# Adding each layer's residual during its last scan, strip by strip, in a four-image convolution block on one core

## Time and profile before

| | |
|---|---|
| median of 3 runs | 2475.09 us (2470.94 to 2479.65) |
| profiled execution | 2475.43 us, span in the trace 2473.6 us |
| PE busy | 2191.7 us (89%) |
| DVE busy | 1443.6 us (58%) |
| ACT busy | 739.2 us (30%) |
| POOL busy | 329.3 us (13%) |
| DMA queue of SP (q1) | 112224 packets, 120.06 MB, 21.1% of the 16 DMA engines' time |

### The profile page before, as it was taken

The page is one execution under the profiler, slowest core; times in us unless marked ns, Lnnn a source line. Parts: engine busy times, 40 slices in busy tenths (PEclk is TensorE's granted clock), DMA queues, the critical chain, the costliest instruction groups (busy, mean ns, idle before and its releaser), DMA issues.

```text
span 2473.6 us, 43617 instructions
## 1 busy us (share of the span) xinstructions
PE 2191.7 (89%) x17396; PEld 1975.7 (80%) x17396; DVE 1443.6 (58%) x3275; ACT 739.2 (30%) x1154; POOL 329.3 (13%) x363
## 2 busy tenths in 40 slices
PE   2999999999999999999999915999999999953786
PEld 2889669489329999999999915999999999952454
DVE  5866776766774444445555586444445555577855
ACT  7923342433545004420035415003440000002442
POOL 2233213123008300000000063000000000000300
PEclk9999999999999999999999967999999999976898
DMA  7600111121355000000000076100000000049935
GB/s 129 107 11 13 16 23 14 17 52 37 58 100 94 1 1 1 1 1 1 1 1 1 1 217 158 22 1 1 1 1 1 1 1 1 1 114 280 304 106 153
DMA packets 119956, 126.72 MB, mean 51 GB/s; under 512 B 50528, under 2 KB 99936, under 8 KB 116960
## 3 DMA queue, kind: packets, MB, share of 16 engines
q1 hardware_dynamic: 112224, 120.06, 21.1%
q10 hardware_dynamic: 7424, 4.06, 0.6%
q0 software_dynamic: 128, 0.01, 0.0%
HBM read 64.47 MB, written 50.33 MB: 46 GB/s over the span
## 4 chain that ended last, share of the span: by engine, by line
PE 83%; DVE 12%; issue 1%; ACT 1%; SPq 1%; DMA 1%; POOL 0%; ACTq 0%; DVEq 0%; POOLq 0%
PE bank L1105 20%; PE bank L1106 18%; PE bank L1107 18%; PE bank L995 10%; PE bank L1066 7%; PE bank L998 4%; DVE stats L1244 4%; PE bank L1069 2%; DVE work L1387 2%; PE bank L1219 2%; PE bank L1010 1%; DVE image L1515 1%; PE bank L1191 1%; DMA band<-in_x 1%; DVE image L1478 1%
## 5 line engine op out<-in xcount | busy, mean ns | idle before, releaser
L1464 DVE TENSOR_TENSOR image<-bank,image 112x128 f32<-112x128 f32 x2032 | 660.4, 325 | 711.4 <-PE bank L1107 711.4
L1105 PE MATMUL bank<-image,scan_area 112*112 112x128 f32 x4064 | 809.5, 280 | 10.4 <-ACT image L849 6.7
L1106 PE MATMUL bank<-image,scan_area 112*112 112x126 f32 x4064 | 771.0, 271 | 0.0
L1107 PE MATMUL bank<-image,scan_area 112*112 112x126 f32 x4064 | 769.7, 270 | 0.0
L1106 PEld LDWEIGHTS bank<-image,scan_area 112*112 112x112 f32 x4064 | 581.3, 176 | 0.0
L1105 PEld LDWEIGHTS bank<-image,scan_area 112*112 112x112 f32 x4064 | 566.3, 175 | 16.2 <-ACT image L849 7.1
L1107 PEld LDWEIGHTS bank<-image,scan_area 112*112 112x112 f32 x4064 | 578.5, 176 | 0.0
L995 PE MATMUL bank<-work 128*128 128x192 f32 x1536 | 307.9, 338 | 28.6 <-DVE work L1387 27.2
L845 ACT COPY work<-image 48x256 f32 x192 | 80.2, 418 | 684.6 <-PE bank L1107 684.3
L995 PEld LDWEIGHTS bank<-work 128*128 128x128 f32 x1536 | 249.9, 194 | 34.2 <-issue 33.1
L783 ACT COPY work<-work 32x1008 f32<-32x1008 f32 x128 | 132.0, 1031 | 298.0 <-PE bank L998 195.1
(11 more groups left out here) (161 smaller groups left out, 1476.4 us busy)
## 6 DMA issues: line engine op xcount, KB each, us to landing
work<-saved SPq DMA_DIRECT2D x64, 384.0 KB, 10.1
saved<-image SPq DMA_DIRECT2D x36, 384.0 KB, 6.9
image<-flat_rows SPq DMA_DIRECT2D x4, 3072.0 KB, 15.9
out<-image SPq DMA_DIRECT2D x8, 1536.0 KB, 8.4
work<-work SPq DMA_DIRECT2D x128, 70.9 KB, 2.8
flat_rows<-image SPq DMA_DIRECT2D x46, 192.0 KB, 5.8
band<-in_x SPq DMA_DIRECT2D x16, 384.0 KB, 5.7
scan_area<-in_x SPq DMA_DIRECT2D x16, 384.0 KB, 5.8
```

Source lines behind the costliest of these rows:

```text
L1105: mm(dst, wt[:, 1], src, start=True, stop=False)
L1106: mm(dst[:, 1:J2, :], wt[:, 0], src[:, 0:J2 - 1, :], start=False, stop=False)
L1107: mm(dst[:, 0:J2 - 1, :], wt[:, 2], src[:, 1:J2, :], start=False, stop=True).then_inc(s_prod[g], 1)
L1464: v.tensor_tensor(line(g, along_w, at), prod, line(g, along_w, src), ALU.add).then_inc(s_state[g], 1)
```

## The change

It does four things. The second exchange is gone: the input of the layer is brought from `saved[0]` in the layout that pass 4 has, in 16 tiles, each a strip of 16 columns j (32 image columns) of one pair and one w, and the sum is made in that layout. As soon as PE has read 8 more columns j of a pair (16 steps; a half strip), POOL adds them to the buffer (112 x 1024 values an add, 28 adds a layer); DVE adds the last half strip after the scan. ACT writes the finished half strips home to `image`: in layer 0 with four 48-partition copies that exchange the layout (`swap_home`), in layer 1 with four 112-partition activations that add the bias and write natural rows (`rows_home`). DVE measures six of the eight half strips inside pass 4, one bn_stats of 128 values after its add in 192 of the 254 slots, beginning 14 steps after the half strip was read, and the last two after the scan. SP saves sums and brings tiles inside pass 4, and in layer 1 it writes each strip of each image to `flat_rows`. Both norms are made once for all four images. The diff, cut to its core:

```diff
-HELD = 2 * (K2 // 8) - GAP
+STRIP = 16
+HALF_STRIP = STRIP // 2
+STRIPS = J2 // STRIP
+TILES = 4 * STRIPS
+LAST = 2 * STRIPS - 1
+PIECE_AT = 14
+ENTRIES = 8 * (LAST - 1) + 4
...
+        def in_image(g, s, half, rows):
+            j = J2 - (half + 1) * HALF_STRIP
+            return image_l[rows, g, s, :, j:j + HALF_STRIP, :].rearrange("p k j b -> p k (j b)")
+        def in_buffer(g, w, half, rows):
+            v = back[(half // 2 * 4 + 2 * g + w) % GAP][rows, :].rearrange("p (k n) -> p k n", k=K2)
+            return v[:, :, (1 - half % 2) * STRIP:(2 - half % 2) * STRIP]
+        def add_half(vector, g, w, half):
+            dst = in_buffer(g, w, half, slice(0, P))
+            return vector.tensor_tensor(dst, in_image(g, w, half, slice(0, P)), dst, ALU.add)
...
             def bring(t):
+                strip, g, w = t // 4, t // 2 % 2, t % 2
+                j = J2 - (strip + 1) * STRIP
+                for h, rows in enumerate((LO, HI)):
+                    src = saved[0][w].rearrange("c (g s k j b) -> c g s k j b", g=2, s=2, k=K2, b=2)
+                    sp.dma_start(back[t % GAP][rows, :].rearrange("p (k n) -> p k n", k=K2),
+                                 src[:, g, h, :, j:j + STRIP, :].rearrange("c k j b -> c k (j b)"))\
+                        .then_inc(s_back[t % GAP], 16)
...
+            for t in range(TILES):
+                summed(sp, t)
+                save(t)
+                if 2 <= t < TILES + 2 - GAP:
+                    done = t - 2
+                    sp.wait_ge(s_gone[done % GAP], 32 * (done // GAP + 1))
+                    sp.wait_ge(s_home, 2 * (done // 4 * 2 + 1) + done // 2 % 2 + 1)
+                    bring(done + GAP)
...
+            def send_rows(strip, b):
+                j = J2 - (strip + 1) * STRIP
+                for h, rows in enumerate((LO, HI)):
+                    sp.dma_start(lines[h, b, :, :, 2 * j:2 * (j + STRIP)],
+                                 image_l[rows, b // 2, b % 2, :, j:j + STRIP, :].rearrange("p k j b -> p k (j b)"))\
+                        .then_inc(s_flat[b], 16)
...
+            for strip in range(STRIPS - 1):
+                for g in range(2):
+                    sp.wait_ge(s_home, HOMES + 2 * (2 * strip + 1) + g + 1)
+                    for t in (4 * strip + 2 * g, 4 * strip + 2 * g + 1):
+                        if t + GAP < TILES:
+                            bring_sum(t + GAP)
+                    send_rows(strip, 2 * g)
+                    send_rows(strip, 2 * g + 1)
+            sp.wait_ge(s_home, 2 * HOMES - 1)
+            send_rows(STRIPS - 1, 0)
+            send_rows(STRIPS - 1, 1)
+            bring_tokens(0)
+            sp.wait_ge(s_home, 2 * HOMES)
+            send_rows(STRIPS - 1, 2)
+            bring_tokens(1)
+            send_rows(STRIPS - 1, 3)
...
-            pool.wait_ge(s_swap, 6 * K2 + 1)
-            for t in range(1, 2 * NBLK, 2):
-                pool.wait_ge(s_back[t % GAP], 32 * (t // GAP + 1))
-                nc.gpsimd.tensor_tensor(dst, piece(image, t), piece(back[t % GAP], t), ALU.add).then_inc(s_kept_p, 1)
+            def add_strips(layer):
+                for half in range(LAST):
+                    for g in range(2):
+                        pool.wait_ge(s_prod[g], (layer * PASSES + 3) * STEPS + 2 * HALF_STRIP * (half + 1))
+                        for w in range(2):
+                            brought(pool, layer, half // 2 * 4 + 2 * g + w)
+                            add_half(nc.gpsimd, g, w, half).then_inc(s_kept_p, 1)
...
+            def swap_home(g, half):
+                for w, to in enumerate((LO, HI)):
+                    for h, of in enumerate((LO, HI)):
+                        last = nc.scalar.copy(in_image(g, h, half, to), in_buffer(g, w, half, of))
+                return last
+            def rows_home(g, half):
+                for b in range(2):
+                    for w in range(2):
+                        dst = in_image(g, b, half, slice(0, P)).rearrange("p k (j w) -> p w k j", w=2)
+                        src = in_buffer(g, w, half, slice(0, P)).rearrange("p k (j b) -> p b k j", b=2)
+                        last = nc.scalar.activation(dst[:, w], src[:, b], ACT.Identity, bias=b2_col[0:P, :], scale=1.0)
+                return last
...
-                with act.Fori(0, K2 - 1) as i:
-                    exchange(True, K2 - 1 - i, 3 * i + n0)
-                exchange(True, 0, n0 + 3 * (K2 - 1))
+                for half in range(LAST + 1):
+                    for g in range(2):
+                        if half < LAST:
+                            act.wait_ge(s_kept_p, layer * 4 * LAST + 4 * half + 2 * g + 2)
+                        else:
+                            act.wait_ge(s_kept_v, layer * 4 + 2 * g + 2)
+                        (rows_home if layer else swap_home)(g, half).then_inc(s_home, 1)
...
                     v.tensor_tensor(line(g, along_w, at), prod, line(g, along_w, src), ALU.add).then_inc(s_state[g], 1)
+                    if scan == PASSES - 1:
+                        strip_piece(layer, 2 * n + g)
+            def strip_piece(layer, slot):
+                half, i = divmod(slot - 2 * PIECE_AT, 4 * HALF_STRIP)
+                half -= 1
+                if not 0 <= half < LAST - 1:
+                    return
+                g, n, b = i // 16, i // 2 % 8, i % 2
+                if i % 16 == 0:
+                    dve.wait_ge(s_home, layer * HOMES + 2 * half + g + 1)
+                v.bn_stats(dst, 128 values of in_image(g, ..., half, ...))
...
+                    add_last(0)
+                    for half in (LAST - 1, LAST):
+                        for g in range(2):
+                            for b in range(2):
+                                for n in range(2):
+                                    last = strip_end(0, g, half, b, n)
+                    group_norm(4, P, ENTRIES)
...
+            add_last(1)
-            for t in range(NBLK):
-                relayout(t)
-            group_norm(6, P, NSTAT, 0, 2)
+            for g in range(2):
+                for half in (LAST - 1, LAST):
+                    dve.wait_ge(s_home, HOMES + 2 * half + g + 1)
+                    for b in range(2):
+                        for n in range(2):
+                            last = strip_end(1, g, half, b, n)
+                last.then_inc(s_taken, 1)
+            group_norm(5, P, ENTRIES)
```

More of the change, by code:

```diff
@@ L276, in build @@
         s_raw = [sem(f"s_raw{i}") for i in range(SAVES)]
-        s_keep = [sem(f"s_keep{g}") for g in range(2)]
+        s_gone = [sem(f"s_gone{i}") for i in range(GAP)]
+        s_home = sem("s_home")
         s_scan_w = sem("s_scan_w")
@@ new lines, in brought, with summed, all_gone @@
+        def brought(eng, layer, t):
+            eng.wait_ge(s_back[t % GAP], 32 * (layer * len(range(t % GAP, TILES, GAP)) + t // GAP + 1))
+        def summed(eng, t):
+            g, w, last = t // 2 % 2, t % 2, t // 4 * 2 + 1
+            eng.wait_ge(s_kept_p, 4 * min(last, LAST - 1) + 2 * g + w + 1)
+            if last == LAST:
+                eng.wait_ge(s_kept_v, 2 * g + w + 1)
+        def all_gone(eng):
+            for i in range(GAP):
+                eng.wait_ge(s_gone[i], 32 * len(range(i, TILES, GAP)))
@@ L1466, in _, with add_last @@
+            def add_last(layer):
+                for g in range(2):
+                    dve.wait_ge(s_state[g], (layer + 1) * PASSES * STEPS + layer + 1)
+                    for w in range(2):
+                        brought(dve, layer, 2 * LAST - 2 + 2 * g + w)
+                        add_half(v, g, w, LAST).then_inc(s_kept_v, 1)
             for layer in range(2):
                 if layer:
-                    def sums(t):
-                        dve.wait_ge((s_kept_v, s_kept_p)[t % 2], t // 2 + 1)
-                        for i in range(2):
-                            for q in range(2):
-                                last = take_stats(P, t // NBLK * 2 + i, t % NBLK * 2 + q, summed(t)[:, i, q])
-                        return last
@@ L1475, in _ @@
-                    for t in range(0, 2 * NBLK, 2):
-                        dve.wait_ge(s_back[t % GAP], 32 * (t // GAP + 1))
-                        dst = piece(image if t < HELD else back[t % GAP], t)
-                        v.tensor_tensor(dst, piece(image, t), piece(back[t % GAP], t), ALU.add).then_inc(s_kept_v, 1)
-                        if t % NBLK:
-                            sums(t - 1)
-                        last = sums(t)
-                        if t % NBLK == NBLK - 2:
-                            sums(t + 1).then_inc(s_stat, 2)
-                        if t == NBLK - 2:
-                            dve.wait_ge(s_stat, X_STATS + NB + 2)
-                            group_norm(4, P, NSTAT, 0, 2)
@@ L1576, in row_norm, with mlp @@
                                     ALU.mult).then_inc(s_ln, 1)
[L1578 removed]
+            def mlp(b, more):
                 for i in range(3):
                     row_norm(b, i)
[L1582 to L1591 removed]
```

268 lines of the change are left out of this document (86 added, 182 removed).

## The result

Four runs of the changed kernel gave a median of **2386.74 us** (2385.31 to 2387.67), four runs of the kernel before 2477.24. The ratio is 0.9635, 95% interval 0.9614 to 0.9655: faster by 3.65%. The profiled execution took 2387.02 us, its span is 2385.2 us, 88.4 less than before.

A forecast was written before the change was run, and what follows sets the result against it. PE's chain (83%) bounds the kernel, mostly scans and convolutions left alone; the gaps between scans can shrink. -54 + 3.6 - 42.5 = -92.9 from 2475.43 gives 2382.5, median 2382 us; own range 2366 to 2400, with two rivals to 2430.

The forecast's parts named there:

- Gap 1, -54: From layer 0's last add to PE's first steps of layer 1: 81.2 us falls to 27, gain 54 us.
- the load of a tile: Residual tile brought in pass 4: 6144 packets of 128 bytes at 15 ns, 5.8 us; four loads and saves 34 us.
- Pass 4, +3.6: Last pass of both layers: layer 0 keeps its slot, layer 1's slot lengthens, adding 3.6 us.
- the slot of 0.694: DVE's time per add in pass 4 beside a busy ACT: layer 0 stays there, layer 1 rises to it from 0.681.
- Statistics in the hole, 0: 192 bn_stats a layer inside pass 4 fit DVE's idle 0.329 us a slot, at cost 0.
- ACT's copies and POOL's adds: In pass 4, per half strip of 21.8 us: ACT 9 or 10.9 us, POOL 9 to 12 us, both covered.
- Gap 2, -42.5: From layer 1's last add to the first output matmul, plus a norm in the output loop: gains 42.5 us.
- 28.8 + 12.1 + 1.6: Gap 2's gains in us: earlier token norm, shorter way to first output matmul, second norm gone from the output loop.
- Short writes at the price of long ones (28.9 ns): Rival, chance 0.13: an image's strip takes 11.1 us, SP falls 41 us behind in layer 1, time 2426.
- at twice that: Rival, chance 0.05: 128-byte writes cost 57.8 ns, SP is 175 us behind at the scan's end, time 2582.
- Overflow of DVE's slots: Rival, chance 0.12: bn_stats costs 0.40 us in pass 4, each slot lengthens by 0.07, 27 us in all, time 2409.
- The work moved: Against a rival, chance 0.03: POOL's adds over 5.4 us fill the half strip, the scan waits, time about 2470.

The follow-up runs named there:

- the repeat: The changed kernel measured again, unedited, in the rounds of the variants beside it: 2385.68 us, ratio 0.9639 to the kernel before.
- the doubled statistics: Against the changed kernel, each of the 192 bn_stats of a layer's last pass taken twice: 2386.68 us, ratio 0.9626 to the kernel before.

## Why the prediction was right, and where it was not

The forecast was 2382, the measurement 2386.7, 4.7 us above it: by the traces 9.6 missed in gap 1 (54 forecast, 44.4 measured), 4.8 found inside the scans, the end right within 0.2. So half of the one error was made good by another.

- **Gap 1, -54: mis-sized by 10.0.** Taken from the forecast's own point, the first pair's start, it came at 35.5 in place of 25.5. Both waits in it hang on one sentence of the prediction, "Tiles 12 to 15 are all there some 3 us before the scan ends". The last one landed 8.5 us behind the end. The term that was mis-sized is the load of a tile: the price of a 128-byte packet read from memory, taken as 15 ns on each of 16 engines, was too low. The first twelve loads give 49.0 x 16 / 36,864 = 21.3 ns, and in the last two strips a tile's packets take 8.2 to 9.7 us where the forecast had 5.8. Four turns of some 10.4 us fill 42 of a strip's 43.5, where I had 34, and with the late start of the last strip (35.5 us before the end) nothing was left for it. Half of a strip's loads also stand behind its later saves: asked for sooner, at the same price of a packet, the last tile landed 13.2 us before the end. With the tiles in time the start comes at 26.1: the remaining 0.6 is bn_aggr, 5.83 for 5.3 (1.46 us over 52 entries, 0.52 over 16). Adds (4.63), statistics (9.6), chain (3.36) and activations (2.54) were right.
- **Pass 4, +3.6: wrong in sign, -2.4 measured** in the two passes together; with the 1.2 us at the turn of layer 1, -1.2 in the scans. I carried the slot of 0.694 beside a busy ACT over to layer 1. The slot stayed at 0.681 with ACT and POOL at work, and layer 0 came down from 0.694 to 0.683 when the exchange went. ACT was also less busy then (36.7 of 100 us, before 50.8; 28.0 in layer 1), in far fewer instructions, so whether the exchange's own accesses or its many instructions had stretched the slot is open.
- **Statistics in the hole, 0: right,** and with room for as many again. "One costs about 0.16 + 0.13 = 0.29 alone and 0.20 behind another" is what the trace shows.
- **ACT's copies and POOL's adds: covered, right.** POOL's adds took 2.34 us, as estimated. The activations home were half as dear as forecast: I had 1.36 us each, the price of an ACTIVATE of 1024 values, 5.4 us for a pair of images. But each moves 512 values: behind the scan the eight of both pairs take 5.42 us, 0.68 each, 2.7 for a pair.
- **Gap 2, -42.5: right** (-42.7), in part because small errors cancel: 28.8 + 12.1 + 1.6 were forecast, 30.0 + 9.8 + 3.0 came. The token norm came at 28.35 for 29.5 (ACT's half-priced activations gave 2.7 us, and about half of it was lost again in the transfers: 12.1 us of packets for the rows of images 0 and 1 where 11.6 were forecast, then 9.6 to the tokens for 8.8). The first output matmul came 60.2 for 57.9 later; there GpSimd's norm of the next image's tokens ran beside DVE (L1622 took 2.39 us in one place and 1.57 in the other). The same stretch in the repeat was 3.8 us shorter, so such meetings move a trace by some us.
- **Rivals.** Short writes at the price of long ones (28.9 ns), or at twice that: both fell. In layer 1's strips four sends, 12,288 packets, run from first packet to last in 12.0 to 13.2 us, 15.6 to 17.2 ns (the profile after and that of the repeat), near the 15 of the forecast. They hold SP 16.2 us, but the sums queued ahead of them are in that time: in the repeat the first of their packets moves 7.1 us after the first send is issued (2035.49, 2028.44). So of the two uses of one price, the writes had it right and the reads did not. The Trainium skill's read-modify-write rule below 512 bytes ("DMA: Bandwidth & Descriptors", Specifications) would make short writes dearer than short reads; at 16 to 17 against 21.3 ns they are cheaper here. Overflow of DVE's slots fell with the doubled statistics. The work moved.

## What to carry to other kernels

When a loop of small dependent steps leaves an engine a hole in each step, work cut to the hole is free, while the same small pieces behind the loop cost more than the large ones that they replace (0.193 us for 128 values, 0.60 for 512); count the hole from start to start, not by durations. When a transfer is cut into short runs so that the work can move, its queue may become the resource that runs out: ask when the *last* piece lands, not what the average load is, and time its packets from the first to the last: the time for which the issuing engine is held is another number. And a wait that is taken away is worth only the distance to the next one; here two more, on TensorE's fill and on the fill's own release, had to go before the first paid.

## What was not expected of the hardware

- Two statistics of 128 values and an add of 128 fit into 0.68 us of VectorE, though their durations sum to 0.93: each next instruction starts some 0.1 us before the one ahead of it is shown as ended.
- The DMA share of the page doesn't give the rate for short packets. Loads of 128 bytes showed a share over 1 at 792 packets a us (above, 760 to 775 us); stores of 128 bytes showed one below it while more of them moved, 1065 a us (changed kernel again, 2037 to 2047 us). By share, packets and time, as the forecast priced its rows, a load would cost 31 ns on an engine and a store 14; by what moved it is 20 and 15.

```profile
q1 hardware_dynamic: 10648, 1.36, 92.4%
```

- GpSimd's fills of 32 x 512 values took 0.48 us alone and 1.3 beside VectorE's one-input operation, which itself went from 3.86 to 4.78 us. In pass 1 the scan's adds took 290 ns beside a busy GpSimd and as much without it (17.84 us for 62 in the kernel before, 860 to 900 us).
